# A fused attention stage: one projection moved by a tile, and the statistics of a finished row block moved and split

## What is computed

```python
x = x + _layernorm(_L0_attn_ref(_layernorm(x), Wq, Wk, Wv, Wo, W_down_kv, W_up_k, W_up_v))
x = x + _layernorm(_L0_ffn_ref(_layernorm(x), ...))      # needs mean and rstd of the new x
...
q = x @ Wq;  latent = (x @ Wk + x @ Wv) @ W_down_kv
k = latent @ W_up_k;  v = latent @ W_up_v                # 16 heads of 8
scores = clip(q k^T / sqrt(128)) * exp(-1e-4 * |i - j|)
out = softmax(scores) @ v;  return out @ Wo
```

## Time and profile before

| | before |
|---|---|
| time, median of 3 executions (lowest to highest) | 1309.95 us (1308.69 to 1311.37) |
| the profiled execution's own time | 1313.5 us |
| its span, first to last instruction | 1311.5 us |
| PE busy, share of the span | 90% |
| DVE | 72% |
| ACT | 70% |
| POOL | 50% |
| attention stage (tiles 0 of batch 0 to its last output) | about 32 to 604 us |

### The profile page before, as it was taken

One profiled execution on the slowest core, in us unless ns is written; L12 is line 12 of the kernel. 1 busy time (PEld: TensorE's weight loads), 2 busy tenths in 40 slices (PEclk: granted clock), 3 DMA queues, 4 the chain that ended last, 5 costly groups with the idle time before them and its releaser, 6 DMA issues. The chain is left out here.

```text
span 1311.5 us, 27435 instructions
## 1 busy us (share of the span) xinstructions
PE 1178.2 (90%) x7367; PEld 531.7 (41%) x7406; DVE 946.8 (72%) x2964; ACT 923.9 (70%) x1411; POOL 652.4 (50%) x1101
## 2 busy tenths in 40 slices
PE   4989999999999999996999468999979999999995
PEld 2222232322222232223666368677633443434442
DVE  5777777777777777775788776466446888888764
ACT  3979999999999999994665590545435666666554
POOL 5425656665666555432555440234123566666534
PEclk9989999999999999997999779999959999999998
DMA  5674565656655555505930011000000000000001
GB/s 155 138 126 87 110 113 105 111 107 111 111 105 110 107 99 107 113 1 137 235 126 0 1 66 65 1 0 0 0 0 1 9 9 16 16 8 17 9 17 33
DMA packets 71699, 87.96 MB, mean 67 GB/s; under 512 B 10368, under 2 KB 65190, under 8 KB 66022
## 3 DMA queue, kind: packets, MB, share of 16 engines
q1 hardware_dynamic: 69326, 85.81, 31.1%
q10 hardware_dynamic: 2296, 1.25, 0.4%
HBM read 63.84 MB, written 31.59 MB: 73 GB/s over the span
## 5 line engine op out<-in xcount | busy, mean ns | idle before, releaser
L562 ACT ACTIVATE a_probs<-a_S 128x1024 f32<-128x1024 f32 x512 | 492.2, 1035 | 45.2 <-DVE a_S L708 40.0
L708 DVE TENSOR_TENSOR a_S<-a_S,a_tables 128x256 f32<-128x256 f32 (+1 forms) x512 | 279.5, 561 | 127.8 <-PE a_S L578 122.7
L585 PE MATMUL a_O<-a_probs,a_V 128*32 128x512 f32 x2048 | 274.8, 609 | 2.4 <-ACT a_probs L562 0.6
L578 PE MATMUL a_S<-a_Qs,a_Ks 48*128 48x512 bf16 x1024 | 182.2, 388 | 19.9 <-ACT a_probs L562 14.2
L578 PEld LDWEIGHTS a_S<-a_Qs,a_Ks 48*128 48x128 bf16 x1024 | 43.8, 93 | 239.2 <-ACT a_probs L562 200.6
L2274 ACT ACTIVATE e_hid<-e_H 128x512 f32<-128x512 f32 x128 | 69.5, 595 | 58.5 <-PE e_H L2389 58.4
L455 POOL CAST a_parts<-a_whole 128x512 bf16<-128x512 f32 x45 | 27.5, 610 | 140.2 <-DVE a_whole L718 140.2
L1960 ACT ACTIVATE g_hid<-g_H,w_b 128x512 f32<-128x512 f32 x64 | 44.0, 687 | 58.1 <-PE g_H L1994 58.1
L2387 PE MATMUL e_H<-e_gated,w_We 64*128 64x512 f32 x256 | 73.2, 648 | 1.3 <-ACT e_hid L2274 1.2
L585 PEld LDWEIGHTS a_O<-a_probs,a_V 128*32 128x32 f32 x2048 | 40.4, 108 | 79.4 <-issue 64.2
L2398 PE MATMUL e_O<-e_hid,w_We 128*64 128x512 f32 x256 | 68.7, 609 | 0.4 <-ACT e_hid L2274 0.4
(11 more groups left out here) (405 smaller groups left out, 2388.1 us busy)
## 6 DMA issues: line engine op xcount, KB each, us to landing
a_parts_dram<-a_parts SPq DMA_DIRECT2D x94, 192.0 KB, 5.7
a_Qs<-a_parts_dram SPq DMA_DIRECT2D x60, 192.0 KB
m_taps_by_step<-h_taps SPq DMA_DIRECT2D x8, 1024.0 KB, 13.2
m_taps<-m_taps_by_step SPq DMA_DIRECT2D x8, 1024.0 KB, 5.2
a_Qs<-a_parts_dram SPq DMA_DIRECT2D x60, 128.0 KB
a_Ks<-a_parts_dram SPq DMA_DIRECT2D x30, 192.0 KB
a_Qs<-a_parts_dram SPq DMA_DIRECT2D x68, 64.0 KB
XY<-L_attn_x SPq DMA_DIRECT2D x16, 256.0 KB, 7.2
```

The costliest lines, as they stand in the source:

```text
L562: act.activation(probs[n % KEPT][:], S[n % RING][:], ACT.Exp).then_inc(exped, 1)
L578: mm = pe.matmul(S[n % RING][:, par, :], Ks[p][rows, pr, kb * P:(kb + 1) * P], Qs[p][Q_OF(kb)][rows, pr, :], start=True, stop=True)
L585: mm = pe.matmul(O[VC * j:VC * (j + 1), :], V[q][:, kb, HG * g + j, :], probs[(2 * m + j // 2) % KEPT][:, j % 2, :], start=(kb == 0), stop ...
L708: v.tensor_tensor(s[:, :, where], s[:, :, where], wide, ALU.mult).then_inc(corrected, 1)
```

## The change

1. **Queries.** PE projects the queries of batch t + 2 behind the score of tile 25 instead of tile 24. DVE still takes them at tile 25.
2. **Statistics.** The four `bn_stats` over `X` of batch t - 2 move from tile 24 to tile 30. Their five small steps move to tile 3 of the next batch, and after the last batch for the last of them.
3. **Written out.** The first small steps at tile 3 exist only from batch 3 on, so batches 2 and 3 are now written out too, and the loop has four turns (batches 4 to 11).

```diff
         def batches(eng, body):
             body(0, 0, first=True)
-            body(1, 1)
-            with eng.Fori(0, (B - 6) // 2) as i:
+            for t in range(1, 4):
+                body(t, t % 2)
+            with eng.Fori(0, (B - 8) // 2) as i:
                 for p in range(2):
-                    body(i * 2 + (p + 2), p)
+                    body(i * 2 + (p + 4), p)
...
-                    if n == 24 and ahead:
+                    if n == 25 and ahead:
                         project(core.Wq, at("q"))
...
-                    if n == 24 and (not isinstance(t, int) or t >= 2):
+                    if n == 3 and (not isinstance(t, int) or t >= 3):
+                        next_norm.moments_of(v, t - 3, None, core.xmean, p=1 - p)
+                    if n == 30 and (not isinstance(t, int) or t >= 2):
                         out_norm.wait_added(v, t - 2)
-                        next_norm.moments_of(v, t - 2, X[:, t - 2], core.xmean, p=p)
+                        next_norm.moments_of(v, t - 2, X[:, t - 2], only_stats=True, p=p)
...
             batches(v, body)
+            next_norm.moments_of(v, B - 3, None, core.xmean, p=1)
             out_norm.wait_added(v, B - 2)
```

## The result

The changed kernel takes **1331.99 us** (median of five executions, 1327.16 to 1335.41), the kernel before 1310.62 us (median of five, 1308.69 to 1311.37): a ratio of 1.0157, 95% interval 1.014 to 1.0174. It is 21.4 us slower; the prediction had 1313.1 and a range up to 1320.0.

What follows compares the result with a forecast made beforehand. The prediction took PE, full without a gap, to bound the kernel. Its terms, -0.7 - 0.8 + 4.2 + 0.4 = +3.1 us on a median of 1309.95, gave 1313.1, with a range from 1309.0 to 1320.0.

Steps and rivals of the forecast that it cites:

- Written-out batches 2 and 3 cost 34.94 - 34.74 = 0.20 more each: Batches 2 and 3, newly written out: each costs a written-out instead of a looped batch's length, +0.4 us together.
- POOL's twelve split operations ... come 0.35 earlier: POOL's split behind the queries: all twelve operations, to the next batch's tiles 3 and 4, come 0.35 us earlier.
- Queries, -0.05 a batch: Tile 25, batches 0 to 13: the output block's copy and everything behind it come 0.05 earlier, -0.7 us in all.
- The statistics at tile 30: Four statistics take 0.86 us at tile 30, where DVE idles 0.74 before tile 31's correction: costed at 0.
- In batches 14 and 15: Nothing is projected there and the statistics delay tile 25: moving them gains 0.4 us in each, -0.8 together.
- The small steps in written-out batches and batch 4, +4.2: Tile 3 of batches 3, 4, 12, 13, 14: DVE's steps stand behind POOL, 0.85 us each, +4.2.
- In the loop the tie went DVE's way: Tile 3, batches 5 to 11: DVE and POOL's cast tie, DVE gets in, 0; locked-out rival +6.1, 1319.2, chance 0.30.
- Behind the last batch, 0: After the last batch: 0.9 us of small steps on DVE fit where it idles 1.59 us, so cost 0.
- The chance of 0.04 for "anything else": Whole kernel: chance of 0.04 left for any outcome besides the forecast and its named rivals; no size given.

Runs made afterwards that it cites:

- experiment 1: Kernel before with only the loop changed: batches 1 to 3 written out and four turns, as in the change; 1322.31 us, ratio 1.0101.
- 16 pads: Kernel before with 16 increments of an unused semaphore on DVE in batch 0, ahead of the loop; a single execution of 1314.73 us.
- 96 pads: Kernel before with 96 increments of an unused semaphore on DVE in batch 0, ahead of the loop; 1310.17 us, ratio 0.9994.
- experiment 4: Kernel before with only the query projection moved behind the score of tile 25; 1312.28 us, ratio 1.0009.
- experiment 7: Kernel before with queries behind the score of tile 25 and batch 1's eight filter steps moved from tiles 29 and 30 to 24; 1305.93 us, ratio 0.9956.
- experiment 9: Experiment 7 plus batches 14 and 15's output statistics and small steps at tile 30, batch 0's small steps at tile 9 instead of 3; 1308.53 us, 0.9986.
- experiment 12: The same kernel as experiment 7, measured once more; 1309.07 us, ratio 0.9979.
- experiment 5: Changed kernel with 72 unused DVE semaphore increments in batch 0, small steps at tile 30 instead of tile 3 of the next batch; 1354.88 us, 1.0322.
- experiment 6: Changed kernel with 72 unused DVE semaphore increments in batch 0, small steps at tile 6 of the next batch instead of tile 3; 1311.36 us, 1.0007.
- experiment 3: Kernel before with 72 pads (increments of an unused semaphore on DVE) in batch 0, ahead of the loop; 1326.73 us, ratio 1.0139.
- experiment 2: Changed kernel with 72 pads (increments of an unused semaphore on DVE) in batch 0, ahead of the loop; 1316.23 us, ratio 1.0039.

## Why the prediction was wrong

**The step that failed is "Written-out batches 2 and 3 cost 34.94 - 34.74 = 0.20 more each".** It priced the written-out batches and put the jumps back at nothing, though the loop behind these batches moves to another place in each program. Batches 2 and 3 did cost about 0.25 each (experiment 1). But the moved loop cost 8.8 us in that experiment and 11.0 in the changed kernel: three waits of 2.96, 2.98 and 2.76 us on issue at the jump back, and the lower clock behind two of them.

Where the loop lies decides it, and one rule fits all kernels. Counted in its own program, DVE's loop runs from instruction 239 to 555 before and from 396 to 717 in the changed kernel. Suppose that code comes in pieces of 128 instructions, and that one piece begins near 708 (the last packet comes some 10 instructions ahead of the jump at 717); then others begin near 196, 324, 452 and 580:

```
kernel           DVE's loop    pieces   stall at a turn
before           239 to 555      3      none
16 pads          255 to 571      3      none
72 pads          311 to 627      4      2.9 us, and 2.1 to 2.7 at the next piece
96 pads          335 to 651      3      none
loop alone       401 to 717      4      2.8 us
changed          396 to 717      4      2.8 to 3.0 us
changed, 72 pads 468 to 789      3      none
```

The loops of experiments 4, 7, 9 and 12 lie where the one before lies, those of 5 and 6 in three pieces (473 to 789 and 468 to 788), and none has a stall. What is measured is that the packets are of 8 KB, that five come in each turn of a loop over four pieces and none, from the second turn on, in a loop over three, and that the last three of the five come 114 to 149 instructions apart. That DVE holds four pieces, one of them fetched ahead, and overwrites the oldest is my reading. It gives the five packets: four pieces and the one behind them, which takes the place of the loop's first. With pieces of 128 the seven loops allow a piece to begin anywhere from 700 to 717; with pieces of 256 no start and no number of them fits all seven. The Trainium skill, "Runtime: NRT & Kernel Launch", section "Instruction fetch mechanics", says that code is fetched ahead in sequence only, and that a taken branch to a target outside the window that is held has to wait for a DMA. The 2.9 us and the packets agree. It gives blocks of 16 KiB and room for 512 instructions. The room agrees with my reading, four times 128; the blocks don't, since the q14 packets are of 8 KB; and a loop of 317 instructions, well inside that room, missed where it touched four pieces. I had not weighed this rule at all: nothing in the trace of before shows a stall, and the place where its absence shows is the DMA view of the loop, without a line for instructions.

Behind attention, where the changed kernel loses 2.5 us, the wait of 4.6 us on issue stands in two kernels alone, the changed one (4.59) and experiment 3 (4.63); in the other twelve it is 1.9 to 2.1, in experiment 1 too, whose loop does stall. So it goes with the place of the code as well, but by which pieces is not shown.

**The second failed step is "POOL's twelve split operations ... come 0.35 earlier"**, which I followed to SP's stores and nowhere else. DVE's small steps stand beside them in batch 1, and the shift from 0.19 ahead of the cast to 0.03 behind it is the same tie that I had worked out for tile 3. Measured: +1.8 us in batches 1 and 2 (experiment 4), 2.8 in experiment 2 and 3.7 in the changed kernel; of the last two some 0.2 is batch 2 being written out. That more than cancels the queries' gain.

**What held**, term by term:
- Queries, -0.05 a batch: the looped batches of experiment 4 are 0.03 shorter. The projection follows the score of tile 25 by 0.32 (0.33 worked out), and DVE takes the queries 0.3 earlier in a looped batch (0.35 worked out; experiment 2, where no stall disturbs). ACT's wait went from tile 25 to the copy and behind it. In looped batch 11 of the changed kernel ACT waits 0.53 before the copy:

```profile
465.76 1.13 PE L615 MATMUL a_M<-a_xnT,Wq 128*128 128x512 f32 x2
...
468.27 0.60 ACT L556 ACTIVATE a_Osb<-a_O 128x512 f32<-128x512 f32 x1 [0.53 <-PE a_O L586]
```

- The statistics at tile 30 take 0.86 as in the earlier trace rows and delay nothing: `472.94 0.86 DVE L150` in the same batch. In batches 14 and 15 they gave back 0.25 each (experiment 9), not 0.4.
- The small steps in written-out batches and batch 4, +4.2: the five batches are 4.9 us longer than before and 4.3 longer than in experiment 1, which has the same batches written out, and moving the steps to tile 6 gave back 4.2 in them. The correction of tile 4 was worked out as 2.6 behind that of tile 3, and is 2.68. The margin was thinner than worked out: the first step starts 0.02 inside the cast, not 0.1. In the loop the tie went DVE's way, as forecast, in all seven batches (no square above 0.16 us), by 0.01 in the rows of batch 11. With distances this small, either side could have come out otherwise; that both came out as forecast is in part luck. The rule of the Trainium skill's "SBUF — State Buffer" that I had cited holds for DVE once more (0.61 and 1.15 behind a POOL operation); POOL again lost only 0.02 in the tie (0.63 for 0.61).
- Behind the last batch, 0: DVE idles 0.96 there where it idled 1.59.

So the terms that I worked out came to +3.1 and measured about +4.5; the other 17 us came from what no term stood for: the loop's place (11.0), the layers behind attention (2.5) and the filter's steps (3.7). The chance of 0.04 for "anything else" was far too small for a change that moves a loop.

## What to carry to other kernels

When a change adds or removes instructions ahead of a hardware loop or inside it, count where the loop lies in each engine's program and look in the DMA view of the loop for instruction packets. If a loop of some 320 DVE instructions turns up with 8 KB packets and waits on issue at its start, a few dozen idle instructions ahead of it can be worth more than any move inside it (here 16 us for 72 pads). A step that starts earlier or later on POOL has to be followed past every small DVE step that may now start behind one of its operations, in the odd batches as well. The version that came out best is the kernel before with the queries behind tile 25 and the filter's steps at tile 24 (0.9956 [0.994, 0.9972], and 0.9979 [0.9961, 0.9998] when measured again).

## What was not expected of the hardware

- The jump back costs in steps: 2.9 us for the first piece and, in experiment 3, 2.1 to 2.7 for the second, 4 to 5 us later. PE's clock then decides how much more: 1.0 to 2.5 us in the batch behind the turn where it fell to 0.50, and nothing behind the turn of the changed kernel where it stayed at 1.00.
- The same layers, far behind attention, take 210.5 us in some profiled executions and 217.7 in others (between DVE's branches at 855.9 and 1073.7 in the kernel before). Over the fourteen profiles the stretch is 210.5 to 212.3 in six, 217.7 to 218.7 in six and 214.8 and 214.9 in two; the kernel of experiments 7 and 12 had 217.8 the first time and 214.9 the second. Windows of it, in the kernel before (217.7) and in experiment 4 (210.5):

```profile
944.00:954.00 10.00, 6.10 (x27) 3.36 (x27) 3.46 (x16) 2.95 (x5) 4.97 (x11) 0.72 0.00 0
954.00:964.00 10.00, 7.77 (x22) 3.97 (x23) 4.88 (x13) 2.82 (x6) 2.85 (x3) 0.50 0.00 0
964.00:974.00 10.00, 6.79 (x21) 2.47 (x21) 6.06 (x24) 3.69 (x8) 2.86 (x7) 0.50 0.00 0
```
```profile
944.00:954.00 10.00, 5.24 (x25) 2.43 (x23) 3.65 (x14) 3.55 (x6) 4.99 (x11) 1.00 0.01 2
954.00:964.00 10.00, 6.62 (x29) 2.79 (x28) 8.55 (x33) 3.55 (x9) 4.06 (x4) 0.83 0.00 0
964.00:974.00 10.00, 7.32 (x32) 3.23 (x33) 5.90 (x20) 3.68 (x8) 2.33 (x6) 0.83 0.00 1
```

The granted clock is at the lower level for some 30 us in the one, from 948 to 979, and for twice 3.4 us in the other. What makes it fall there in some executions is open. It is one reason why medians of kernels that differ by a microsecond can't be told apart.
